# A gated cross-attention and mixture-of-experts layer: the calls of the last two batches and the early tiles in a new order, and the last down weights' low half on VectorE

## The reference

```python
x = x + jnp.tanh(g_xattn[0]) * _L0_xattn_ref(_layernorm(x, axis=-1), ctx_1024, L0_xattn_w_q, L0_xattn_w_kv, L0_xattn_w_out, L0_xattn_b_out)
x = x + jnp.tanh(g_ffn[0]) * _L0_ffn_ref(_layernorm(x, axis=-1), L0_ffn_W1, L0_ffn_W2, L0_ffn_Wr)
...
logits = jnp.einsum('btd,ed->bte', x, Wr)
probs = jax.nn.softmax(logits / TEMPERATURE, axis=-1)
topk_vals, topk_idx = jax.lax.top_k(probs, TOPK)
router_weights = topk_vals / topk_vals.sum(-1, keepdims=True)
...
h = jax.nn.silu(jnp.einsum('btd,efd->btef', x, W1))
y = jnp.einsum('btef,edf->bted', h, W2)
out = jnp.einsum('bte,bted->btd', gate, y)
```

## Time and profile before

| | us |
|---|---|
| median of 3 runs | 528.88 |
| lowest and highest run | 528.67, 530.03 |
| the profiled execution, its own time | 530.4 |
| its span (first to last instruction) | 528.7 |
| TensorE busy | 486.9 (92%) |
| VectorE busy | 363.8 (69%) |
| ScalarE busy | 371.2 (70%) |
| GpSimd busy | 369.9 (70%) |

### The profile page before, as it was taken

The page is one execution under the profiler, slowest core; times in us unless marked ns, Lnnn a source line. Parts: engine busy times, 40 slices in busy tenths (PEclk is TensorE's granted clock), DMA queues, the critical chain, the costliest instruction groups (busy, mean ns, idle before and its releaser), DMA issues.

```text
span 528.7 us, 17694 instructions
## 1 busy us (share of the span) xinstructions
PE 486.9 (92%) x6692; PEld 436.4 (83%) x6692; DVE 363.8 (69%) x866; ACT 371.2 (70%) x577; POOL 369.9 (70%) x414
## 2 busy tenths in 40 slices
PE   2889689999999999999688999989999999999993
PEld 2877568888888878888468899979999999999993
DVE  5799899898988989998887757553344443444431
ACT  1788989999899989988764577544555655556551
POOL 5369779798999999899968766564554645455432
PEclk9999989999999999999989999998999999999998
DMA  7953416154360725325073638886888888788712
GB/s 289 398 195 95 167 38 204 51 185 140 99 208 34 243 67 182 124 95 195 24 268 110 255 118 303 251 254 150 260 226 245 241 226 265 212 256 239 211 22 31
DMA packets 35061, 94.87 MB, mean 179 GB/s; under 512 B 4507, under 2 KB 24475, under 8 KB 27645
## 3 DMA queue, kind: packets, MB, share of 16 engines
q1 hardware_dynamic: 25812, 82.79, 45.2%
q0 software_dynamic: 8592, 10.81, 11.9%
q10 hardware_dynamic: 576, 0.14, 0.1%
HBM read 74.45 MB, written 19.28 MB: 177 GB/s over the span
## 4 chain that ended last, share of the span: by engine, by line
PE 66%; POOL 12%; DVE 9%; ACT 5%; issue 5%; DMA 3%; POOLq 0%; SPq 0%; ACTq 0%; DVEq 0%
PE st_bank L1707 20%; PE j_bank L1707 15%; PE o_bank L1707 14%; PE j_bank L1852 4%; POOL pT L618 3%; POOL stage L663 3%; PE max_pair L1908 2%; PE j_bank L1713 2%; PE st_bank L1929 2%; POOL table L637 2%; PE j_bank L1811 2%; DMA stage<-in_w 2%; PE max_pair L1970 1%; DMA w2s<-in_wq 1%; PE j_bank L1876 1%
## 5 line engine op out<-in xcount | busy, mean ns | idle before, releaser
L1541 DVE SCALAR_TENSOR_TENSOR hT<-hf,h_scale,hT 128x512 f16<-128x512 f32 x78 | 58.9, 758 | 87.2 <-ACT hT L1016 87.1
L1707 PE MATMUL st_bank<-xsT,w_tile 128*128 128x128 f16 x1872 | 113.3, 221 | 2.1 <-DVE xsT L1535 1.4
L1707 PEld LDWEIGHTS st_bank<-xsT,w_tile 128*128 128x128 f16 x1872 | 109.6, 99 | 3.0 <-DVE xsT L1535 1.6
L730 POOL DMA_INDIRECT out<-yt,row_of x39 | 62.7, 1607 | 57.0 <-DVE yt L1550 42.3
L1010 ACT ACTIVATE hf<-st_bank,z_scale 128x512 f32<-128x512 f32 x78 | 52.9, 678 | 45.2 <-PE st_bank L1707 39.2
L618 POOL TENSOR_TENSOR pT<-pT 120x512 f16<-120x512 f32 x64 | 77.3, 1223 | 7.3 <-ACT pT L884 7.1
L1707 PE MATMUL o_bank<-w2s,hT 128*128 x600 | 69.7, 273 | 0.3 <-DVE yt L1550 0.3
L1016 ACT ACTIVATE hT<-hf,h_scale 128x512 f16<-128x512 f32 x78 | 56.3, 722 | 10.5 <-PE o_bank L1707 4.2
L1707 PEld LDWEIGHTS o_bank<-w2s,hT 128*128 128x128 f16 x600 | 57.6, 98 | 7.1 <-issue 0.8
L883 ACT ACTIVATE pT<-st_bank,exp_bias,logit_scale 120x512 f32<-120x512 f32 x64 | 50.0, 781 | 14.0 <-PE st_bank L1932 12.7
L663 POOL TENSOR_SCALAR stage<-stage,upw 128x512 f32<-128x512 f32 x32 | 56.5, 1766 | 4.1 <-ACT w_hi L983 4.1
(11 more groups left out here) (226 smaller groups left out, 1022.7 us busy)
## 6 DMA issues: line engine op xcount, KB each, us to landing
w_tile<-w_split SPq DMA_DIRECT2D x39, 1024.0 KB, 6.3
stage<-in_w SPq DMA_DIRECT2D x16, 1024.0 KB, 5.1
w_split<-w_hi SPq DMA_DIRECT2D x8, 512.0 KB, 2.8
w_split<-stage SPq DMA_DIRECT2D x8, 512.0 KB, 3.8
out<-x SPq DMA_DIRECT2D x17, 128.0 KB, 3.2
xin<-in_x SPq DMA_DIRECT2D x8, 256.0 KB
w2s<-in_wkv SPq DMA_DIRECT2D x2, 1024.0 KB, 11.9
xres<-in_x SPq DMA_DIRECT2D x16, 128.0 KB, 2.1
```

The source lines that it names most:

```text
L730: pool.indirect_dma_start(out=out[0:rows], out_offset=bass.IndirectOffsetOnAxis(row_of[:, t:t + 1], 0), in_=yt[t % XG][:], in_offset=None, ...
L1541: nc.vector.scalar_tensor_tensor(out=hT[par][:, 1, 4 * a:4 * a + 4, :], in0=hf[par][:, 512 * a:512 * a + 512].rearrange("p (c n) -> p c n" ...
L1707: ins = pe.matmul(out, lhs[i](a), rhs[i](c), start=(i == 0 and a + c == 0), stop=(i == n - 1 and a == 1))
```

## The change

The calls of the last two periods that have work, and all calls of the tiles 0 to 9, are taken out of the lists; the lists run to period 5 (GpSimd's to -1 in its own count), and what followed is written out call by call, in a new order, on TensorE, VectorE, ScalarE and GpSimd. SP's list is the same. The job of the early entries' transposes (`FE`) moves back in each of the three orders of jobs that hold it. The last expert's down weights get all four low quarters from VectorE, where GpSimd made two. The semaphore `tables_done` (after the gates) becomes `units_done` (after the scales of the up product), so ScalarE's `tile_hidden` waits for less. The number of spare matmuls goes from 18 + 44 to 14 + 18.

```diff
-PRODUCT_ORDER = (("Awq", 4), ("Q3", 2), ("X2T", -1), ("Q1", 2), ("LG", -1), ("FE", -2), ("Ka", 2), ("Vb", 1), ("OT0a", 0),
-                 ("MT1", 1), ("OT1b", 0), ("Kb", 2), ("A3", 2), ("OT0b", 0), ("Q2", 2), ("RK", -1), ("PJ1", 0),
+PRODUCT_ORDER = (("Awq", 4), ("Q3", 2), ("X2T", -1), ("Q1", 2), ("LG", -1), ("Ka", 2), ("Vb", 1), ("OT0a", 0),
+                 ("MT1", 1), ("OT1b", 0), ("FE", -2), ("Kb", 2), ("A3", 2), ("OT0b", 0), ("Q2", 2), ("RK", -1), ("PJ1", 0),
...
-            for p in range(-8, B + 3):
+            for p in range(-8, 0):
...
-                split_low(E - 1 if p == 0 else E, 1, 2)
-                split_low(E - 1 if p == 0 else E, 1, 3)
...
+            p_low(6, 2, 1)
+            norm2_factors(5)
+            scatter(4, 1)
...
-                act.wait_ge(tables_done, 1 if isinstance(t, int) and t < EARLY else 2)
+                act.wait_ge(units_done, 1 if isinstance(t, int) and t < EARLY else 2)
...
-            for p in range(-2, B + 21):
+            for p in range(-2, 6):
...
+            exps(6, 3, 1)
+            o_high(6, 1, 0)
+            norm2(5)
+            split_high(7, 0, 0)
...
-            def by_tile(vec, dst, n):
+            def by_tile(vec, dst, n, late=None):
...
-                chain.link(nc.vector.tensor_reduce(dst, by_expert[:, 0:n], AX.X, ALU.add))
+                ins = nc.vector.tensor_reduce(dst, by_expert[:, 0:n], AX.X, ALU.add)
+                if late is None:
+                    chain.link(ins)
+                else:
+                    ins.then_inc(units_done, 1)
+                    dve.wait_ge(units_done, 1 + late)
...
-                by_tile(h8, h_scale[:, c], c.stop - c.start)
+                by_tile(h8, h_scale[:, c], c.stop - c.start, late)
...
-            for p in range(-3, B + 25):
+            for p in range(-3, 6):
...
+            o_low(6, 1, 1)
+            max_rows(7, 1)
+            row_ids(4, 0)
+            tile_experts(4, 0)
...
+            add_residual(6, 0)
+            tile_scales(7, 0, 0)
+            tile_low(7, 0)
...
+            o_low(7, 0, 0)
+            o_low(7, 1, 1)
+            split_low(7, 1, 0)
+            split_low(7, 1, 1)
+            split_low(7, 1, 2)
+            split_low(7, 1, 3)
+            o_low(7, 0, 1)
...
-            for p in range(-4, B + 35):
+            for p in range(-4, 6):
...
+            out_product(6, 1, 1)
+            col_scores(7, 3)
+            out_product(6, 0, 0)
+            out_product(6, 0, 1)
+            values(7, 1, 1)
+            tile_T(7, 0)
+            tile_T(7, 1)
+            spare("OT1a", 7, 14)
+            values(7, 2, 0)
+            spare("OT1a", 7, 18)
+            tile_up(7, 0, 0)
```

More of the change, by code:

```diff
@@ new lines, in _ @@
+            add_residual(5, 0)
+            norm_o(6, 1, 1)
+            max_rows(7, 0)
+            weight_scales(7)
+            norm_o(6, 2, 0)
+            count_tiles(4, 0, 0)
+            count_tiles(4, 0, 1)
+            count_tiles(4, 0, 2)
+            row_max(7, 2)
+            norm_o(6, 2, 1)
+            split_low(7, 0, 0)
+            o_low(6, 1, 0)
+            v_low(7, 0)
+            norm_o(6, 3, 0)
+            split_low(7, 0, 2)
+            norm2_rows(5)
+            norm_o(6, 3, 1)
@@ L2031, in _ @@
                 logits(p - 1)
-                find_T(p - 2, 0)
                 k_product(p + 2, 0)
@@ L2106, in _ @@
                 q_product(p + 3, 0)
                 col_scores(p + 2, 0)
+            values(6, 3, 0)
+            norm2_T(5)
+            values(6, 3, 1)
+            row_scores(7, 3)
+            logits(5)
+            v_product(7, 1)
+            o_T(6, 0, 0)
+            col_scores(7, 1)
+            max_T(7, 1)
+            values(7, 0, 0)
+            o_T(6, 1, 1)
+            find_T(4, 0)
+            values(7, 0, 1)
+            o_T(6, 0, 1)
+            col_scores(7, 2)
+            ranks(5)
@@ new lines, in _ @@
+            values(7, 3, 0)
+            values(7, 3, 1)
+            norm2_T(6)
+            logits(6)
+            o_T(7, 0, 0)
+            o_T(7, 1, 1)
+            tile_up(7, 1, 1)
+            o_T(7, 0, 1)
+            ranks(6)
+            out_product(7, 1, 0)
+            out_product(7, 1, 1)
+            out_product(7, 0, 0)
+            tile_T(7, 2)
+            out_product(7, 0, 1)
+            tile_T(7, 3)
+            tile_down(7, 0)
+            tile_up(7, 2, 0)
+            tile_T(7, 4)
@@ new lines, in _ @@
+            tile_down(7, 1)
+            tile_T(7, 5)
+            norm2_T(7)
+            tile_up(7, 2, 1)
+            logits(7)
+            tile_up(7, 3, 0)
+            tile_up(7, 3, 1)
+            ranks(7)
+            tile_down(7, 2)
+            tile_up(7, 4, 0)
+            tile_T(7, 6)
+            tile_T(7, 7)
+            tile_up(7, 4, 1)
+            tile_down(7, 3)
+            tile_up(7, 5, 0)
+            tile_up(7, 5, 1)
+            tile_down(7, 4)
+            tile_T(7, 8)
+            tile_up(7, 6, 0)
@@ L2109, in _ @@
+            tile_up(7, 6, 1)
+            tile_down(7, 5)
+            tile_up(7, 7, 0)
+            tile_up(7, 7, 1)
+            tile_T(7, 9)
+            tile_up(7, 8, 0)
+            tile_down(7, 6)
+            tile_up(7, 8, 1)
+            tile_up(7, 9, 0)
+            find_T(7, 1)
+            tile_T(7, 10)
+            tile_down(7, 7)
+            tile_up(7, 9, 1)
+            tile_down(7, 8)
             pe.wait_ge(experts_done, 2)
```

394 lines of the change are left out of this document (228 added, 166 removed).

## The result

The changed kernel took **540.3 us** in the median of 4 runs (537.89 to 542.74), the kernel before 529.45 beside it (528.67 to 530.07): a ratio of 1.0216, 95% interval 1.0166 to 1.0266. It is slower by 2.2%, 16 us above the forecast and outside the range.

What follows compares the result with a forecast made beforehand. TensorE was taken to bound the kernel, except around 250 to 290 us, where VectorE and GpSimd are fuller. The terms -3.7 - 1.0 + 2.1 - 2.8 + 0.6 = -4.8 us gave a median of 524.1 us, range 521.7 to 528.6.

Steps and rivals of the forecast that it cites:

- What bounds the kernel: Whole kernel: TensorE sets the end, except from about 250 to 290 us, where VectorE and GpSimd are fuller.
- Part 2: Up to batch 7's second score product: moved count costs nothing, less low clock; 1.0 us earlier, bounds 3.4 earlier, 1.0 later.
- Part 3: Late row ids delay GpSimd's gathers and the subtractions behind them, so `values(7, 1, 0)` waits: +2.1 us, bounds 0 and +2.5.
- Part 1: Where early tiles meet the loop: tile 10's earlier transpose and splits shorten the 9.47 us pass, -3.7 us.
- Part 4: `values(7, 1, 0)` to first up half: GpSimd rid of down weights, 9.6 us instead of 12.4; -2.8, between -3.5 and -1.0.
- Part 5: Four down-weight splits on VectorE ahead of `o_low(7, 0, 1)`, at 0.74 us each: +0.6 us, from 0 to 3.2 more.
- VectorE is stretched: Rival: the four splits meet GpSimd's elementwise work and take the long time, 3.2 us more, 527.3; chance 0.12.
- The clock stays low: Rival: granted clock below about 0.8 between 270 and 280 us, +6.6 us, 530.7; chance 0.10.

Runs made afterwards that it cites:

- ninth kernel: The eighth kernel with VectorE's tile count put back behind the weight scales and one more normalization; 531.39 us against 528.25 for before, ratio 1.0057.
- tenth kernel: The eighth kernel with Part 3 alone put back (row ids and tile experts late); 533.65 us, ratio 1.0064 against before.
- thirteenth: The eighth kernel unchanged, run once more for a profile of another execution; 527.45 us.
- eighth: The changed kernel with Parts 2 and 3 undone, batch 6's router factors ahead of unit 3's subtractions on GpSimd; 524.5, 524.88, 532.81 and 536.12 us.
- second profile: The kernel before, unchanged, profiled once more; that execution took 525.43 us.
- the three edits: Changed kernel, on GpSimd: scatter ahead of batch 5's factors, two gathers behind two subtractions, batch 6's factors between scatter and subtractions; 535.11 us against 526.67, 1.0162.
- sixth: The kernel before with batch 5's router factors ahead of a scatter on GpSimd, putting it directly ahead of two subtractions; 528.77 us, 1.0038.

## Why the prediction was wrong

**What bounds the kernel** held: TensorE, and the stretch from 250 on, where VectorE is full. The loss lies there.

**Part 2 is the step that failed.** I costed the moved count at nothing, bounds -0.8 to +1.0, and took 1.0 us of gain from the clock. The ninth kernel gives +6.1 to +7.9 by fronts, of which 0.8 to 1.8 is idle time. The hole that I put at about 3 us was 5.38 there and 7.88 in the changed kernel. I had read that the lower clock followed broken work, and then expected one hole in place of three to give some of it back. By windows of 1 us, the low stretch of the changed kernel did begin earlier, at about 257.1 instead of 261.9, and part of it fell into the wait, as I expected; but it ended at about 274.1, where before it had ended at 268.8. The row that should have warned me was in the prediction: 1.08 us for a weight scale beside a subtraction. For the count's own operations beside subtractions my upper bound had 1.0 us in all.

**A step that I did not price at all:** where GpSimd's DMAs come to stand. The change puts a scatter directly ahead of two subtractions at two places (the factors of batches 5 and 6 moved away from between them). I read the first as "waits about 1 us longer, which VectorE covers" and passed over the second. In profiled fronts these two places are worth up to 5.1 and 5.3 us; the medians bear out the second (4.8) and not the first.

**Part 3** was right in its mechanism: GpSimd idle (11.09 us) until the row ids, and a wait of 2.50 us on TensorE where I said some 2. Its own term was sized well: from the front's start to `values(7, 1, 0)` the tenth kernel took 48.9 us, the thirteenth 46.7 and the eighth 47.4, so +1.5 to +2.2. The whole edit cost +3.0 to +4.9 instead of +2.1, with a starving `ratio` and a lower clock that I had not priced.

**Part 1** was mis-sized: -0.5 in two profiles, at most -2.4 by the runs, instead of -3.7. Of the 9.47 us, 1.6 was the lower clock of that one execution (48 matmuls in 4.48 us; 2.85 in the other profile), and "next late there is nothing" was false: `yt` and the issue of the next transposes were late next, by 0.95 and 0.54 us.

**Part 4** held where Part 3 was undone: from `values(7, 1, 0)` to the first up half the thirteenth kernel took 9.51 us, where I said 9.6 (12.39 before, 12.11 in the second profile), and the eighth 9.52. In the changed kernel it was 12.02, with the 3.46 us of waiting behind the starving operation on the tiles' scales.

```profile
272.93 0.53 PE L1850 MATMUL o_bank<-v,pT 120*128 120x65 f16 x12
...
282.44 1.51 PE L1850 MATMUL st_bank<-xsT,w_tile 128*128 128x128 f16 x24 [0.94 <-DVE xsT L1619]
```

**Part 5** was right about the splits. From the first up half to tile 0's down product the thirteenth kernel took 18.15 us against 17.08 and 16.60 before. TensorE waited there 0.35 us for VectorE's `oT`, the place that I priced at +0.6, but ahead of that 0.92 for `o` (0.35 in the second profile of before) and 0.95 for `xn2T` (no wait before), which no part had priced. By these two stretches the two parts gave -1.8 to +0.1, over two profiles of before and two of the eighth kernel, instead of -2.8 + 0.6 = -2.2. The whole front's -2.6 (74.35 against 76.9) has 1.5 us of clock in it; the eighth's 76.2 gives -0.7. The four splits took the short time of the earlier trace rows, as this line of VectorE in the changed kernel shows (four in a row, start and total):

```profile
309.04 2.73 DVE L1457 SCALAR_TENSOR_TENSOR w2s<-stage,upw,w2s 128x512 f16<-128x512 f32 x4
```

**The rivals.** "VectorE is stretched" named a real mechanism but looked at the four large splits, which met no GpSimd work; it was the operations of 0.2 us that were stretched, on the path of the values. "The clock stays low" had its sign and its place a window too late (0.79 from 270 to 280, 0.50 before that), and a price of 6.6 us for holes that I did not expect to be so long. Neither reached 540, and no case of mine joined the two: a stretched small operation makes a hole, and the low clock comes on top. That is the case that came, though how much of the loss is the clock's own was not separated: with matmuls in the hole the front fell by 3.3 us and the time did not. By fronts the 14.6 us divide so: the three edits take back 10.8 (91.5 to 80.7: starving, and the gathers ahead of the subtractions), undoing the rest of Parts 2 and 3 another 4.5 to 6.4 (to 76.2 or 74.35; the late count alone was 6.1 to 7.9), and what is left had saved 0.7 to 2.6. The single prices add up to more than that; behind two neighbouring holes the low clock is counted once in the whole and twice in the parts, which is my reading of it and was not tried by itself.

## What to carry to other kernels

Where one engine is full and a second one feeds it, look in a new order at what stands directly ahead of each pair of long GpSimd operations, and at which VectorE operations begin there: here operations of 0.2 to 0.3 us took 2.7 to 3.0. Price a hole ahead of TensorE with the clock that follows it, from windows of the same stretch. Look behind the mended stretch too: here the gain was whole only after a gather further on had moved. And profile the kernel before twice before a pass of it is taken as a saving: here 1.6 of 9.47 us belonged to one execution.

## What the runs showed of the hardware

**A VectorE operation can be passed over.** Five times in the three kernels shown (changed, sixth, tenth) an operation that elsewhere takes 0.2 to 0.3 us (128 x 8, 128 x 4 and 128 x 2 elements, with one or two tensor inputs) began during a GpSimd indirect DMA that two subtractions followed at once. They took 2.98, 2.85, 2.72, 2.93 and 2.85 us and ended when both subtractions were done. Where it began during the subtractions themselves, in the ninth kernel, two operations in a row took 1.16 and 1.08, one subtraction each. The Trainium skill (SBUF — State Buffer, Who interferes with whom) says that whoever issues first holds the shared ports for the whole instruction and the other waits. The 1.16 and 1.08 agree with that; that an operation waits through a DMA's issue and two further instructions queued behind it goes beyond what the page says. Other VectorE operations that began earlier in the same issues took their usual 0.15 to 0.23 us, so which ones are held, and why a waiting one is not served in between, is not shown.

**The clock behind a hole.** In the ninth kernel's profile, around and behind 5.38 us of waiting, TensorE's granted clock was 0.50, its lower level, over the whole window from 260 to 270, and the front lost 8.8 us to the clock, with 10.6 us of idle time. Without the late count the same front lost 0.0 and 3.2 us to it in two profiles, with 9.8 and 8.8 us of idle time in shorter holes. With 110 unread matmuls in the changed kernel's hole it was 1.00 up to 260 and 0.74 in the next window.
